# Top-16 attention in a small language-model tower: one block for preparation and attention

## The reference

```
pos = conv1d(x, pos_w (c,1,3), depthwise, padding 1)
x = x + pos + pos_b
q, k, v = split(x @ qkv_w.T + qkv_b)          # then split into 8 heads
logits = q * c**-0.5 @ k.T                    # (16, 1024, 1024)
idx = top_k(logits, 16)
attn = softmax over the 16 chosen logits
out = sum of attn * v[idx], heads joined
return out @ wo_w.T + wo_b                    # and h = h + this
```

## Time and profile before

| | us |
|---|---|
| median of 3 runs (lowest to highest) | 1556.85 (1556.62 to 1558.61) |
| the profiled execution | 1553.99 |
| its span, first to last instruction | 1552.3 |
| VectorE busy / TensorE busy | 1156.7 / 1206.6 |
| ScalarE / GpSimd busy | 731.2 / 686.2 |
| mean granted clock | 0.900 |

### The profile page before, as it was taken

How to read it: one execution, slowest core, us unless ns; L and a number is a source line. 1 busy time by engine, 2 the same in 40 slices (tenths; PEclk the granted TensorE clock), 3 DMA queues, 4 the chain that set the end, 5 groups by cost and what they waited for, 6 DMA issues and landing times. The chain is left out here.

```text
span 1552.3 us, 30152 instructions
## 1 busy us (share of the span) xinstructions
PE 1206.6 (78%) x10544; PEld 829.6 (53%) x10552; DVE 1156.7 (75%) x2187; ACT 731.2 (47%) x1106; POOL 686.2 (44%) x608
## 2 busy tenths in 40 slices
PE   5867999998699878788777777777777776759761
PEld 3734666665489767534444444444444444557651
DVE  5666566563635697478999999999999994657983
ACT  4243434432135411167777767767676773002540
POOL 2213134230376641235555556555555553214655
PEclk9887999999699989699999999999999997956995
DMA  4044000000268400000000000000000000012772
GB/s 129 1 119 136 2 2 2 3 2 25 69 171 225 126 22 1 1 0 1 1 0 0 0 0 0 0 0 0 0 0 0 0 1 1 3 36 77 223 217 78
DMA packets 83498, 65.00 MB, mean 42 GB/s; under 512 B 14058, under 2 KB 73860, under 8 KB 83140
## 3 DMA queue, kind: packets, MB, share of 16 engines
q1 hardware_dynamic: 62980, 46.86, 10.9%
q0 software_dynamic: 4096, 8.40, 1.9%
q10 hardware_dynamic: 16320, 8.40, 1.8%
HBM read 43.70 MB, written 22.28 MB: 43 GB/s over the span
## 5 line engine op out<-in xcount | busy, mean ns | idle before, releaser
L1697 POOL TENSOR_TENSOR ta_ex<-ta_ex,ta_left 128x1024 f32<-128x1024 f32 x128 | 301.7, 2357 | 290.4 <-ACT ta_left L1640 290.4
L1541 PE MATMUL ta_ps_s<-ta_kT,ta_qz 128*128 (+1 forms) x512 | 277.2, 669 | 35.1 <-ACT ta_ex L1624 33.8
L1572 PE MATMUL ta_ps_t<-consts,ta_ex 128*128 128x128 f32 x1024 | 141.4, 282 | 107.3 <-POOL ta_ex L1697 47.6
L1572 PEld LDWEIGHTS ta_ps_t<-consts,ta_ex 128*128 128x128 f32 x1024 | 112.9, 144 | 175.0 <-POOL ta_ex L1697 137.8
L1728 DVE MAX8 ta_top<-ta_ps_s 128x8 f32<-128x1024 f32 x128 | 156.3, 1221 | 45.4 <-PE ta_ps_s L1541 45.1
L1624 ACT ACTIVATE ta_ex<-ta_ps_s,ta_ntop 128x1024 f32<-128x1024 f32 x128 | 142.7, 1115 | 62.6 <-DVE ta_left L1734 51.1
L1541 PEld LDWEIGHTS ta_ps_s<-ta_kT,ta_qz 128*128 128x128 f32 x512 | 94.2, 204 | 124.3 <-issue 110.4
L1734 DVE MATCH_REPLACE8 ta_left<-ta_top,ta_ps_s 128x1024 f32<-128x1024 f32 x128 | 155.3, 1213 | 0.0
L1739 DVE MAX8 ta_top<-ta_left 128x8 f32<-128x1024 f32 x128 | 154.6, 1208 | 0.0
L1744 DVE MATCH_REPLACE8 ta_left<-ta_top,ta_left 128x1024 f32<-128x1024 f32 x128 | 154.6, 1207 | 0.0
L1640 ACT ACTIVATE ta_left<-ta_left,ta_ntop 128x1024 f32<-128x1024 f32 x128 | 146.3, 1143 | 1.1 <-DVE ta_left L1744 0.3
(11 more groups left out here) (629 smaller groups left out, 2588.8 us busy)
## 6 DMA issues: line engine op xcount, KB each, us to landing
l1f_arena<-in_L_ffn_W_dram SPq DMA_DIRECT2D x46, 256.0 KB
l3e_packed<-l3f_packed SPq DMA_DIRECT2D x64, 160.0 KB, 2.7
l3f_rows<-l1f_zero SPq DMA_DIRECT2D x2, 2048.0 KB, 14.0
l3e_x<-l3f_rows SPq DMA_DIRECT2D x32, 128.0 KB, 2.8
l3e_outs<-l3e_y ACTq DMA_DIRECT2D x32, 128.0 KB
l1f_rows<-l1f_zero SPq DMA_DIRECT2D x2, 1472.0 KB, 9.5
l1f_arena<-l1f_rows SPq DMA_DIRECT2D x46, 64.0 KB
l1e_outs<-l1e_y ACTq DMA_DIRECT2D x46, 64.0 KB
```

Of the source, the lines that this page charges most:

```text
L1541: ins = pe.matmul(ps_s[:, i % 2, half * BANK:(half + 1) * BANK], qz[:, odd, h, :], kT[:, grp, bass.ds(at.key0[i // PAIR] + half * BANK, BA ...
L1572: ins = pe.transpose(ps_t[:, j * P:(j + 1) * P], ex[:, i % 4, j * P:(j + 1) * P], m.ident)
L1697: pool.tensor_tensor(ex[:, i % 4, :], ex[:, i % 4, :], left[:, i % 4, :], ALU.subtract).then_inc(kept, 1)
```

## The change

It removes the block `topk_prepare` and spreads its work. The DMAs and the padding become `fetch` and `pad`, which the layernorm block runs on SP and behind GpSimd's second power. The convolution, the bias columns and the values go to the head of `topk_attend`. The order of the projections is new, one half of the queries is spread as soon as its projection is copied, and the scores of items 0 and 1 come after four projections, those of items 2 and 3 after the values. The eight value tiles go into one PSUM area of two banks and are copied at once. The value bias is no longer added to the values (L1414 and L1580 go): it is multiplied with `wo` once and added to the output bias. The convolution of the second sequence stands ahead of VectorE's first MAX8. A spin of four stands ahead of the projections.

```diff
-def layernorm(nc, m, name, src, dst, dstT, gain=None, shift=None, loaded=None, fetch=None):
+def layernorm(nc, m, name, src, dst, dstT, gain=None, shift=None, loaded=None, fetch=None, pad=None):
...
+            if pad is not None:
+                pad(pool)
...
+        def fetch(sp):
+            sp.dma_start(r.posw[:, :], w["L2_ffn_pos_w"].rearrange("d a k -> d (a k)")).then_inc(loaded, 16)
+            sp.dma_start(r.posb[:, :], col(w["L2_ffn_pos_b"]), allow_slow_non_contiguous=True).then_inc(loaded, 16)
+            sp.dma_start(r.qkvb[:, :], row(w["L2_ffn_qkv_b"])[:, 0:2 * D]).then_inc(loaded, 16)
+            sp.dma_start(r.bv[:, :], col(w["L2_ffn_qkv_b"])[2 * D:3 * D, :], allow_slow_non_contiguous=True).then_inc(loaded, 16)
             sp.dma_start(r.wo_b[:, :], row(w["L2_ffn_wo_b"])).then_inc(loaded, 16)
+        def pad(pool):
             pool.memset(r.v[:, :, :, TW:TW + 1], 1.0)
+            pool.memset(r.wpad[:, :, :, :], 0.0).then_inc(padded, 1)
+            pool.memset(r.brow[:, :, :, :], 0.0).then_inc(padded, 1)
+            pool.wait_ge(loaded, 80)
+            pool.wait_ge(padded, 2)
             for kind in range(2):
...
+            pool.tensor_scalar(r.posw[:, 1:2], r.posw[:, 1:2], 1.0, None, ALU.add)
+
+        layernorm(nc, m, "ln_l2f", m.h, m.xn, m.xnT, fetch=fetch, pad=pad)
+        topk_attend(nc, m, r)
...
-            kind, grp, half = [(0, 0, 0), (0, 1, 0), (1, 0, 0), (1, 0, 1), (1, 1, 0), (1, 1, 1), (0, 0, 1), (0, 1, 1)][k]
+            kind, grp, half = [(0, 0, 0), (1, 0, 0), (1, 0, 1), (0, 1, 0), (1, 1, 0), (1, 1, 1), (0, 0, 1), (0, 1, 1)][k]
...
-                        pe.matmul(out, r.xc[:, t], m.wqkv3[:, 2, :], start=True, stop=False)
-                        ins = pe.matmul(out, m.one[0:1, :], r.qkvb[:, 2 * D:3 * D], start=False, stop=True)
+                        ins = pe.matmul(out, r.xc[:, t], m.wqkv3[:, 2, :], start=True, stop=True)
...
-            for k in range(8):
-                if k >= 4:
-                    pe.wait_ge(proj_done, k - 3)
+            def project_first(k):
                 project(0, k, start_banks[k % 4]).then_inc(proj_ready, 1)
+
+            for n in range(4):
+                pe.matmul(ps_p[:, n:n + 1], r.brow[0:1, n // 2, n % 2, :], m.one[0:1, 0:1], start=True, stop=True)
+            pe.matmul(ps_p[0:1, P:2 * P], r.bv[:, :], m.wo[:, :], start=True, stop=True).then_inc(b_ready, 1)
+            spin(pe, m, ps_s[:, 0, 0:BANK], 4)
+            pe.wait_ge(conv_step, 3)
+            for k in range(3):
+                project_first(k)
+            pe.wait_ge(b_in, 2)
+            project_first(3)
+            pe.wait_ge(proj_done, 3)
+            for i in range(2):
+                logits(place(pe, 0), i, True)
+            for k in range(4, 8):
+                pe.wait_ge(proj_done, k - 3)
+                project_first(k)
+            pe.wait_ge(proj_done, 6)
+            for t in range(CH):
+                ins = pe.matmul(ps_t[:, t * P:(t + 1) * P], r.xc[:, t * P:(t + 1) * P], m.wqkv3[:, 2, :], start=True, stop=True)
+            ins.then_inc(v_ready, 1)
+            for i in range(2, AHEAD):
+                logits(place(pe, 0), i, True)
+            pe.wait_ge(q_in, 1)
+            pe.wait_ge(v_done, 1)
             pe.wait_ge(proj_done, 8)
-            for i in range(AHEAD):
-                logits(place(pe, 0), i)
+            pe.wait_ge(conv_step, 6)
             steps(pe, step)
...
-            for k in range(8):
+            def keep_projection(k):
                 act.wait_ge(proj_ready, k + 1)
                 copy_projection(0, k, start_banks[k % 4]).then_inc(proj_done, 1)
+
+            act.wait_ge(b_in, 1)
+            for k in range(5):
+                keep_projection(k)
+            shift(place(act, 0), 0)
+            keep_projection(5)
+            all_exp(place(act, 0), 0)
+            shift(place(act, 0), 1)
+            keep_projection(6)
+            keep_projection(7)
+            act.wait_ge(v_ready, 1)
+            act.activation(r.v[:, 0:CH, :, 0:TW], ps_t[:, :].rearrange("p (t h d) -> p t h d", t=CH, h=TH), ACT.Copy).then_inc(v_done, 1)
+            act.wait_ge(v_done, 1)
             act.wait_ge(v_in, 1)
             fetch_values(0)
-            shift(place(act, 0), 0)
-            all_exp(place(act, 0), 0)
-            shift(place(act, 0), 1)
             steps(act, step)
...
-            pool.wait_ge(proj_done, 2)
-            query(place(pool, 0), 0)
+            for grp in range(2):
+                pool.wait_ge(proj_done, (1, 4)[grp])
+                pool.tensor_tensor(qz[:, 0, 4 * grp:4 * grp + 4, :], qT[:, grp, 0:P].unsqueeze(1).broadcast_to([P, 4, P]),
+                                   m.quarter.unsqueeze(2).broadcast_to([P, 4, P]), ALU.mult).then_inc((q_first, q_in)[grp], 1)
...
+            for b in range(B):
+                x, z = b * S, (b + 1) * S
+                dve.tensor_scalar(r.xc[:, x:z], m.xnT[:, x:z], r.posw[:, 1:2], r.posb[:, 0:1], ALU.mult, ALU.add).then_inc(conv_step, 1)
...
+                if b == 0:
+                    dve.wait_ge(b_ready, 1)
+                    dve.tensor_copy(r.bpad[:, :, :].rearrange("p a b -> p (a b)"), ps_p[:, 0:4]).then_inc(b_in, 1)
+                    dve.tensor_tensor(r.wo_b[:, :], r.wo_b[:, :], ps_p[0:1, P:2 * P], ALU.add).then_inc(b_in, 1)
             first_max(place(dve, 0), 0)
```

More of the change, by code:

```diff
@@ L1360, in stage_l2_ffn @@
         r.bpad = sb("bpad", [P, 2, 2])
-        r.wo_b, r.qkvb = sb("wo_b", [1, D]), sb("qkvb", [1, 3 * D])
-        topk_prepare(nc, m, r, w)
-        topk_attend(nc, m, r)
[L1366 to L1386, removed]
@@ L1403, in _ @@
-        @block.tensor
-        def _(pe):
-            pe.wait_ge(pool_step, 6)
-            for n in range(4):
-                ins = pe.matmul(ps_b[:, n:n + 1], brow[0:1, n // 2, n % 2, :], m.one[0:1, 0:1], start=True, stop=True)
-            ins.then_inc(b_ready, 1)
-            pe.wait_ge(dve_step, 4)
-            for t in range(CH):
-                if t >= 2:
-                    pe.wait_ge(v_done, t - 1)
-                pe.matmul(ps_v[:, t % 2, 0:D], r.xc[:, t * P:(t + 1) * P], m.wqkv3[:, 2, :], start=True, stop=False)
-                pe.matmul(ps_v[:, t % 2, 0:D], m.one[0:1, :], r.qkvb[:, 2 * D:3 * D], start=False, stop=True).then_inc(v_ready, 1)
@@ L1416, in _ @@
-        @block.scalar
-        def _(act):
-            for t in range(CH):
-                act.wait_ge(v_ready, t + 1)
-                act.activation(r.v[:, t, :, 0:TW], ps_v[:, t % 2, 0:D].rearrange("p (h d) -> p h d", h=TH), ACT.Copy).then_inc(v_done, 1)
-        @block.vector
-        def _(dve):
-            steps = [0]
-            def link(ins):
-                steps[0] += 1
-                ins.then_inc(dve_step, 1)
-                dve.wait_ge(dve_step, steps[0])
-            dve.wait_ge(loaded, 64)
-            mid = posw[:, 1:2]
-            link(dve.tensor_scalar(mid, mid, 1.0, None, ALU.add))
-            for b in range(B):
-                a, z = b * S, (b + 1) * S
-                link(dve.tensor_scalar(r.xc[:, a:z], m.xnT[:, a:z], mid, posb[:, 0:1], ALU.mult, ALU.add))
-                link(dve.scalar_tensor_tensor(r.xc[:, a + 1:z], m.xnT[:, a:z - 1], posw[:, 0:1], r.xc[:, a + 1:z], ALU.mult, ALU.add))
-                link(dve.scalar_tensor_tensor(r.xc[:, a:z - 1], m.xnT[:, a + 1:z], posw[:, 2:3], r.xc[:, a:z - 1], ALU.mult, ALU.add))
-            dve.wait_ge(b_ready, 1)
-            dve.tensor_copy(r.bpad[:, :, :].rearrange("p a b -> p (a b)"), ps_b[:, 0:4])
+                                 m.wqkv3[:, kind, :].rearrange("p (gh d) -> p gh d", d=TW))
@@ L1492, in topk_attend @@
             sem(x) for x in ("values_done", "o_ready", "o_turned", "oT_in", "out_ready", "out_in", "out_used"))
+        b_ready, b_in, conv_step, q_first, v_ready, v_done = (
+            sem(x) for x in ("b_ready", "b_in", "conv_step", "q_first", "v_ready", "v_done"))
         block = ctx.enter_context(nc.Block())
@@ L1532, in project, with logits @@
                 return pe.matmul(bank, r.wpad[:, kind, grp, :], r.xc[:, tokens], start=True, stop=True)
-            def logits(at, i):
+            def logits(at, i, begin=False):
                 h, odd, n = i % TH, (i // TH) % 2, at.item0 + i
                 grp = h // 4
-                if h == 0:
+                if begin:
+                    pe.wait_ge(q_first, 1)
+                elif h == 0:
                     pe.wait_ge(q_in, at.tile0 + (i // TH + 1))
```

23 lines of the change are left out of this document (12 added, 11 removed).

## The result

Median 1537.57 us (1534.25 to 1540.06, 4 runs) against 1556.73 us (1554.87 to 1558.61, 4 runs) for the kernel before: ratio 0.9872 [0.984, 0.9905], 19.2 us less. The profiled execution took 1540.06 us (span 1538.3, clock 0.892) against 1553.99 (1552.3, 0.900): 13.9 us less. In every ratio here, executions more than 1.5% above the fastest of their kernel are left out; a median takes in all.

What follows compares the result with a forecast made beforehand. VectorE bounds the loop (busy 549.44 of 568 us), after 31.0 us with almost no item work. Gains of 16.1 (item 2 earlier) + 2.5 (late bias matmuls) = 18.6 us, from median 1556.85, gave 1538.2; range 1533.5 to 1544.5.

Steps and rivals of the forecast that it cites:

- VectorE's first scores: At the stage's start: first MAX8 of item 0 at 646.9 instead of 666.00, 19.1 us earlier.
- three signs of being wrong: Layernorm ending on GpSimd by over 2 us; items 3 or 4 waiting for ScalarE over 1 us each; loop idle moving over 5 us.
- Loads and pad under the layernorm: DMAs and padding hidden under the layernorm: pad over at 634.4 (633.0 to 636.6), cost nothing; normalising loses nothing to 0.5 us.
- a late pad: At the layernorm's end: if GpSimd made no headway beside VectorE's normalising, the pad ends near 635.3, costing 0.3 us.
- Start of the joint block: Head of attention block: convolution 3.6 us to 638.9; small matmuls, product and half-clock spin end last, at 641.3.
- Clock: TensorE's clock at the stage's start: 0.50 in the spin, 1.00 from the first projections on.
- rival 2: Start: clock rises only after the first logits, 10 passes costing 4.3 us; gain 14.3, time 1542.5; chance 0.18.
- Value tiles: Eight tiles before item 2's scores take 8 x 0.41 = 3.3 us; 3.0 us given back, item 2 16.1 us earlier.
- Late bias matmuls: Late value pairs in the first tile: 0.82 us less each, three of them shortening VectorE's waits, 2.5 us gained.
- Rival 3: Loop behind the first tile: lower granted clock makes VectorE wait, 0.2 us per 0.01 in each 80; slower; chance 0.03.

Runs made afterwards that it cites:

- e4: Changed kernel with the five small DMAs and the padding moved from the layernorm back to the head of the attention block; median 1540.2 us, ratio to before 0.9809.
- e2: Changed kernel with GpSimd's clearing of the value tile held until VectorE's first convolution pass is over; median 1540.0 us, ratio to before 0.9853.
- c1: The changed kernel run again unaltered; median 1545.81 us over 12 runs, beside 1562.32 us for the kernel before.
- e6: Changed kernel with item 2's scores ahead of the value tiles and two ScalarE exponentials ahead of its value copy; median 1537.19 us, ratio to before 0.9773.
- e1: Changed kernel with the one-row bias matmul put back behind every value tile; median 1555.9 us, ratio to before 0.9907.
- b1: Kernel before with only the value bias folded into the output bias; median 1537.8 us, ratio to before 0.9898.
- c2: Repeat of the changed kernel with the edits of e2 and e6 together; median 1543.52 us over 6 runs, ratio to before 0.9893.
- e10: Changed kernel with the value bias added again by a 128-row matmul per value tile; median 1552.35 us from 2 executions, ratio to before 0.9951.
- e9: Changed kernel with two spin matmuls behind four of every eight loop items; median 1548.56 us, ratio to before 0.9932.

## Why the prediction was right, and where its steps were not

It held: 1538.2 against 1537.57 us. The mechanism (VectorE's first scores, then its waits for TensorE) was right. That the medians agree to 0.6 us is luck in part: the profiled execution was forecast at 1535.4 and took 1540.06, and within the start several errors cancel. None of the three signs of being wrong came: GpSimd was done before the layernorm's end, VectorE did not wait at items 3 and 4, and its idle time in the 568 us of the loop went from 18.6 to 20.8 us. Step by step:

- **Loads and pad under the layernorm:** right, over 2.0 us before the layernorm, and with the 0.85 us of the later start taken off at 633.5, nearer to the short end (633.0) than to the chosen 634.4. But "taken as nothing" was wrong for the normalising: 5.01 us instead of 4.19 beside the memsets and copies (4.19 again in e4, without them), and the layernorm 0.5 longer, the upper end that was written down. The Trainium skill (GPSIMD Engine Reference, § 8 Key points) has GpSimd and VectorE contend when VectorE runs in a two-port mode. The trace agrees that the two meet: the three memsets took 1.77 us instead of 1.42, and VectorE lost 0.82. The 0.3 us that had been worked out for a late pad did not come.
- **Start of the joint block:** the spin, forecast to end last, did not. At first it ran at full clock (637:638), ended at 641.07, and the convolution at 641.6, 5.0 us after the block's start where 3.6 were counted. The small matmuls, the product and the spin took 4.4 us together where 6.0 were counted. The missing term is GpSimd's memset beside VectorE's first pass (e2). From the layernorm's first statistics the projections began at 17.2 us; 17.7 was forecast. So two errors, a spin counted too slow and a convolution counted too fast, left the start 0.5 us early, the longer layernorm included.
- **Clock:** forecast full from the first projection, granted after the second. This is a small part of rival 2 (four passes 1.8 us longer); c1 and e6 show that it can also be full from the first, and item 0 is then 2.2 us earlier. Item 0: 19.1 + 0.5 (start) − 1.8 (clock) = 17.8; measured 17.6. From the layernorm's last copy to the first MAX8 it took 12.9 us; 11.6 was forecast.
- **Value tiles:** 3.3 us were counted, taking 0.41 a tile, which is one matmul's step beside a one-row one. Alone a tile takes 0.24, in all 1.95; the wait at item 2 was 1.33 us, not 3.0. This cancelled what item 0 had lost: 16.2 against 16.1.
- **Late bias matmuls:** 0.82 us a pair was counted as gone, but from the pair's first pass to the next matmul it took 0.44 us (663.83 to 664.27) instead of 1.56 (690.16 to 691.72), so 1.1 us went each time. VectorE's waits of 1.28, 2.49 and 1.28 became none, 1.80 and none, where 0.5, 1.7 and 0.5 were forecast. From item 2 to item 11 4.1 us were gained, not 2.5. This is the mis-sized term of the sum. The fold as a whole was counted at 5.8 us (3.3 in the first tiles, 2.5 later) and is worth 10 (e1, b1).
- **Rival 3, the loop's clock:** the price is real, and greater than was read from single windows of the loop: 0.2 us in each 80 for 0.01 of clock, which is 1.4 us over the stage, against 24.2 us between 0.98 and 0.90, or 3.0 for each 0.01 (c1, c2). But the kernel before moves with the clock just as much (1542 to 1572 us), and at equal clock the result stands (18.6 us). In the profiled pair, at 0.94 and 0.92, the stretch behind item 11 took back 3.6 of its 20.3 us.

## What to carry to other kernels

Where one engine is full in the loop, look at what stands between the stage's start and its first instruction, and order the other engines' work by what that engine waits for next; here, by the items, the order alone was worth 2.5 us, the work moved under another stage 7.6, and the removed operations 10. When a small operation is removed, count the time between its neighbours with and without it, not its own duration: a bias matmul of one row made its neighbour slow too. When times scatter by more than the effect, compare both kernels at fixed places of their traces and at the same clock.

## What the runs showed of the hardware

- One-row matmuls between 128-row ones: at full clock a value tile takes 0.24 us alone, 0.45 with a 128-row bias matmul (e10), and 0.83 with a one-row one when the tile stands behind another such (e1, and 690.89 to 691.72 in before). At half clock it takes 4.70/8 = 0.59 alone (b1) and 1.45 with a one-row one (before). In e1 the clock fell from 1.00 to 0.50 among such tiles with TensorE busy all the time; in e10 it stayed at 1.00.
- VectorE's fp32 tensor_scalar of 128x1024 took 2.31 us while GpSimd cleared 128x2048 (1.81 us), and 0.81 without it. The Trainium skill (SBUF — State Buffer, Who interferes with whom) has VectorE and GpSimd contend in VectorE's two-port mode, with the second to issue fully blocked until the first ends. The trace agrees in the order and roughly in the size: the pass was issued 0.04 us behind the memset (636.66 and 636.62) and ended 0.54 us behind its end; a full block and then 0.81 us of work would have ended it 0.81 behind.
- Beside VectorE's two-input passes it is the other way round: those keep 1.28 us, and GpSimd's copy takes 1.37 us (e4) where another of the same shape, 1.0 us earlier, took 0.28. A clearing there costs neither anything: 1.28 and 1.81 us (e2).
- The stretch from item 11 to the third layer took 569 to 570 us in the seven traces with a mean clock of 0.98 or 0.99 and 586 to 594 in the six with 0.90 to 0.94, with the same loop in all. Executions of one kernel on one chip (before, 17 of them) took 1542 us at a mean clock of 0.920 and up to 1572 at 0.884. Filling TensorE's pauses gave 0.99 and still 591.9 us (e9).
